# A gated cross-attention and int8 feed-forward block: rows of four batches rounded on GpSimd, turned in 32x32 blocks on VectorE and carried by DMA

## What is computed

```python
def _quant_per_tensor(x):
    scale = jnp.maximum(jnp.max(jnp.abs(x)), MIN_RANGE) / QP      # QP = 127
    return (_ste_round(x / scale), scale)
def _qlinear(x2d, w, b):
    xq, sx = _quant_per_tensor(x2d)
    wq, sw = _quant_per_tensor(w)
    return (jnp.matmul(xq, wq.T) + b[None, :]) * (sw * sx)
x = x + jnp.tanh(g_xattn[0]) * _L0_xattn_ref(_layernorm(x), ctx_1024, ctx_1024, ...)
h = gelu(_qlinear(_layernorm(x), w1, b1))                         # 512 -> 2048
x = x + jnp.tanh(g_ffn[0]) * _qlinear(h, w2, b2)                  # 2048 -> 512
```

## Time and profile before

| | us |
|---|---|
| median of 3 runs | 366.87 (366.56 to 367.69) |
| profiled execution | 366.82 |
| its span, first to last instruction | 365.0 |
| PE busy in the span | 351.0 |
| VectorE busy | 330.1 |
| ScalarE busy | 284.5 |
| GpSimd busy | 119.8 |

### The profile page before, as it was taken

One profiled execution on the slowest core, in us unless ns is written; L12 is line 12 of the kernel. 1 busy time (PEld: TensorE's weight loads), 2 busy tenths in 40 slices (PEclk: granted clock), 3 DMA queues, 4 the chain that ended last, 5 costly groups with the idle time before them and its releaser, 6 DMA issues.

```text
span 365.0 us, 6668 instructions
## 1 busy us (share of the span) xinstructions
PE 351.0 (96%) x2424; PEld 240.0 (66%) x2424; DVE 330.1 (90%) x630; ACT 284.5 (78%) x493; POOL 119.8 (33%) x178
## 2 busy tenths in 40 slices
PE   8889989999999899999999999999999999999995
PEld 2556767887886785454535545454648888888884
DVE  3699999999999969999999888987779999999996
ACT  1476879889886966889859988789799999999520
POOL 2645578688789690079000000430000000000000
PEclk9999999999999999999999999999999999999998
DMA  7999988565311454767738850000192999995225
GB/s 224 370 404 405 396 312 303 193 221 195 116 55 64 171 187 160 291 287 289 330 129 360 331 233 0 3 0 0 58 422 58 371 398 428 423 417 244 95 117 230
DMA packets 22963, 84.78 MB, mean 232 GB/s; under 512 B 2129, under 2 KB 11857, under 8 KB 14482
## 3 DMA queue, kind: packets, MB, share of 16 engines
q1 hardware_dynamic: 22272, 83.89, 59.6%
q10 hardware_dynamic: 658, 0.46, 0.4%
HBM read 54.99 MB, written 29.36 MB: 231 GB/s over the span
## 4 chain that ended last, share of the span: by engine, by line
PE 57%; DVE 20%; ACT 8%; POOL 5%; issue 5%; DMA 3%; SPq 1%; DVEq 0%; ACTq 0%; POOLq 0%
PE PS L1491 19%; PE PS L1446 18%; DVE hmax L1046 6%; PE PS L1327 6%; PE PS L1266 5%; ACT ring L709 5%; DMA X<-in_x 3%; DVE hmax L839 2%; PE PS L1308 2%; PE PS L1275 2%; DVE ring L1023 2%; PE PS L1287 2%; POOL ring L493 2%; POOL w1q L495 1%; PE PS L1298 1%
## 5 line engine op out<-in xcount | busy, mean ns | idle before, releaser
L689 ACT ACTIVATE ring<-PS,bias,sc 128x512 f32<-128x512 f32 x128 | 96.3, 783 | 22.5 <-DVE hmax L1046 6.8
L1446 PE MATMUL PS<-mid,w1q 128*128 128x512 bf16 x500 | 109.8, 379 | 0.6 <-ACT ring L689 0.3
L1446 PEld LDWEIGHTS PS<-mid,w1q 128*128 128x128 bf16 x500 | 48.4, 98 | 58.4 <-ACT ring L689 1.5
L1046 DVE TENSOR_REDUCE hmax<-ring 128x1 f32<-128x2048 f32 x30 | 67.5, 2279 | 5.6 <-ACT ring L689 5.6
L709 ACT ACTIVATE ring<-ring,sc 128x2048 int16<-128x2048 f32 x29 | 55.6, 1987 | 0.0
L1491 PE MATMUL PS<-w2q,ring 128*128 128x256 f16 x336 | 39.0, 273 | 0.0
L1491 PEld LDWEIGHTS PS<-w2q,ring 128*128 128x128 f16 x336 | 32.9, 98 | 4.0
L1174 DVE SCALAR_TENSOR_TENSOR X<-PS,sc,X 128x512 f32<-128x512 f32 x48 | 35.3, 746 | 0.0
L1327 PEld LDWEIGHTS PS<-w2q,ring 128*128 128x128 f32 x256 | 29.2, 192 | 6.7 <-issue 6.7
L1327 PE MATMUL PS<-w2q,ring 128*128 128x128 f32 x256 | 30.5, 277 | 0.4 <-DVE w2q L879 0.4
L1266 PE MATMUL PS<-ring 128*128 128x129 f32 x256 | 30.0, 275 | 0.7 <-ACT ring L612 0.7
(11 more groups left out here) (151 smaller groups left out, 593.4 us busy)
## 6 DMA issues: line engine op xcount, KB each, us to landing
spilled_hidden<-ring SPq DMA_DIRECT2D x20, 1024.0 KB, 3.9
ring<-spilled_hidden SPq DMA_DIRECT2D x20, 1024.0 KB, 9.1
ring<-in_ctxT SPq DMA_DIRECT2D x8, 1024.0 KB, 4.9
ring<-in_ctx SPq DMA_DIRECT2D x8, 896.0 KB, 9.3
X<-in_x SPq DMA_DIRECT2D x7, 1024.0 KB, 9.6
out<-X SPq DMA_DIRECT2D x7, 1024.0 KB, 9.6
ring<-in_w1T SPq DMA_DIRECT2D x4, 1024.0 KB, 13.2
ring<-in_w2T SPq DMA_DIRECT2D x8, 512.0 KB, 3.4
```

The costliest lines, as they stand in the source:

```text
L689: nc.scalar.activation(ring[:, s * CH + c, (h % CH) * N:(h % CH + 1) * N], PS[:, hidden_bank(s, h), :], ACT.Gelu, scale=SC1, bias=bias1[:, ...
L1046: V.tensor_reduce(hmax[:, bass.ds(CH * g + c, 1)], ring[:, s * CH + c, :], AX.X, ALU.max, apply_absolute_value=True).then_inc(hm_done, 1)
L1446: mm = nc.tensor.matmul(PS[:, hidden_bank(s, h), :], w1v[:, k, h * P:(h + 1) * P], xqT[:, s, k, :], start=(k == 0), stop=(k == NH - 1))
```

## The change

For groups 4 to 7 (`CARRIED` is 4) the rows take another way. GpSimd normalises them in float32, adds MAGIC and takes it off (`round_rows`), once group g - 3 is spilled and its maxima are taken. VectorE turns them in 32x32 blocks by four instructions (`turn_x`), between maxima 1 and 2 of group g - 2. SP writes them to HBM (`write_rows`) behind the spills of group g - 2 and fetches them from there in four DMAs (`fetch_rows`), each into 32 partitions, so that every feature stands on its partition. The matmuls of these groups read them in place as [4 x 4 x 32] columns (`turned_block`). TensorE's transposes and VectorE's quantising and copies go for these groups. For group 3 they stay. ScalarE's wait for maxima, at g >= 3, asks for those of group g - 3 only, and falls away below.

```diff
--- before.py
+++ after.py
@@ -46,6 +46,7 @@
     out_v = out.rearrange("b (p i) d -> b p i d", i=NT)
     w1_v = w1T.rearrange("(k p) (a n) -> p k a n", p=P, a=PIECES // NH)
     w2_v = w2T.rearrange("(q k p) n -> q p k n", p=P, q=PIECES)
+    carry = nc.dram_tensor("carried_rows", (B, NT, 32, NT, D), BF16, kind="Internal").ap()
     spill = nc.dram_tensor("spilled_hidden", (SPILLED * CH, P, CW), F32, kind="Internal").ap()
 
     with ExitStack() as es:
@@ -122,6 +123,21 @@
         bpt = mid[:, 1536:2048]
         S_sb = mid[:, 2048:3072].rearrange("p (j e) -> p j e", e=P)
         xqT = mid[:, :].bitcast(BF16).rearrange("p (s k n) -> p s k n", s=SLOTS, k=NH)
+        xqB = mid[:, :].bitcast(BF16).rearrange("p (s t m) -> p s t m", s=SLOTS, t=NT)
+        CARRIED = SLOTS + 1
+
+        def turned_block(g, k):
+
+            return xqB[:, g % SLOTS].rearrange("p t (k i w) -> p k i t w", k=NH, i=NT)[:, k]
+
+        def rounded_rows(g):
+
+            return ring[:, g % SLOTS * CH + 2, 0:CW // 2].bitcast(BF16)
+
+        def turned_rows(g):
+
+            return ring[:, g % SLOTS * CH + 2, CW // 2:CW].bitcast(BF16)
+
         ring16 = ring[:, :, :].bitcast(I16)
         hq = w1q[:, :].bitcast(F16).rearrange("p (c k n) -> p c k n", c=CH, n=N)
         blocks_h = w1q[:, :].bitcast(F16).rearrange("p (c k n) -> p c k n", c=CH, n=HN)
@@ -199,6 +215,9 @@
         w2_step, w2y_done, w2q_done = (sem(n) for n in ("w2_step", "w2y_done", "w2q_done"))
         xs_step, xs_pow, scales = (sem(n) for n in ("xs_step", "xs_pow", "scales"))
         y_done, xq_done, xT_done, xqT_done = (sem(n) for n in ("y_done", "xq_done", "xT_done", "xqT_done"))
+        rounded_g, rounding_g, turned_x = (sem(n) for n in ("rounded_g", "rounding_g", "turned_x"))
+        written = [sem(f"written{g}") for g in range(B)]
+        moved = [sem(f"moved{g}") for g in range(B)]
         h_done, gelu_done, hm_done = (sem(n) for n in ("h_done", "gelu_done", "hm_done"))
         spilled = [sem(f"spilled{s}") for s in range(SLOTS)]
         back_in = [[sem(f"back_in{s}_{c}") for c in range(CH)] for s in range(SLOTS)]
@@ -369,10 +388,31 @@
                 load_w2(q)
 
 
+            def write_rows(g):
+
+                sp.wait_ge(turned_x, NT * (g - CARRIED + 1))
+                sp.dma_start(carry[g].rearrange("t r a m -> (t r) a m"),
+                             turned_rows(g).rearrange("p (a m) -> p a m", a=NT)).then_inc(written[g], 16)
+
+            def fetch_rows(g):
+
+                sp.wait_ge(written[g], 16)
+                sp.wait_ge(h_done, KH * (g - SLOTS + 1))
+                for a in range(NT):
+                    sp.dma_start(xqB[32 * a:32 * a + 32, g % SLOTS],
+                                 carry[g].rearrange("t r a m -> a r t m")[a]).then_inc(moved[g], 16)
+
             for g in range(SPILLED):
                 for c in range(CH):
                     sp.wait_ge(gelu_done, KH * g + (c + 1) * KH // CH + len(H_BANK))
                     sp.dma_start(spill[g * CH + c], ring[:, (g % SLOTS) * CH + c, :]).then_inc(spilled[g % SLOTS], 16)
+                    if c == 0 and g > 2:
+                        fetch_rows(g + 1)
+                if g >= 2:
+                    write_rows(g + 2)
+            fetch_rows(SPILLED + 1)
+            write_rows(B - 1)
+            fetch_rows(B - 1)
 
             for p in range(B):
                 if p + SLOTS < B:
@@ -541,6 +581,24 @@
                 nc.gpsimd.tensor_scalar(w2q[:, q * CW:(q + 1) * CW], w, -MAGIC, 1.0,
                                         ALU.add, ALU.mult).then_inc(w2q_done, 1)
 
+
+            def round_rows(g):
+
+                n = g - CARRIED
+                pool.wait_ge(spilled[g % SLOTS], 16 * CH * (g // SLOTS) + 1)
+                pool.wait_ge(hm_done, CH * (g - SLOTS + 1) + 1)
+                y = ring[:, g % SLOTS * CH + 3, :]
+                for i in range(NT):
+                    nc.gpsimd.tensor_scalar(y[:, i * D:(i + 1) * D], X[:, g, i, :], nmean[:, 4 * g + i:4 * g + i + 1],
+                                            rstd[:, 4 * g + i:4 * g + i + 1], ALU.add, ALU.mult).then_inc(rounding_g, 1)
+                pool.wait_ge(rounding_g, (NT + 1) * n + NT)
+                nc.gpsimd.tensor_scalar(y, y, MAGIC, 1.0, ALU.add, ALU.mult).then_inc(rounding_g, 1)
+                pool.wait_ge(rounding_g, (NT + 1) * (n + 1))
+                nc.gpsimd.tensor_scalar(rounded_rows(g), y, -MAGIC, 1.0, ALU.add, ALU.mult).then_inc(rounded_g, 1)
+
+            pool.wait_ge(xs_step, 8)
+            for g in range(CARRIED, B):
+                round_rows(g)
 
             pool.wait_ge(w2q_done, CH)
             pool.wait_ge(h_done, KH * (B - 2))
@@ -679,8 +737,8 @@
                 act.wait_ge(spilled[s], 16 * CH * turn + 1)
                 for h in range(KH):
                     c = h // (KH // CH)
-                    if h == 0:
-                        act.wait_ge(hm_done, turn * (CH * SLOTS) + 1)
+                    if h == 0 and g >= SLOTS:
+                        act.wait_ge(hm_done, CH * (g - SLOTS + 1) + 1)
                     if g == 1 and h == KH // 2:
                         act.wait_ge(xT_done, 3)
                     if g == 2 and h % (KH // CH) == 0:
@@ -1026,6 +1084,14 @@
                 dve.wait_ge(y_done, 4 * g + 4)
                 V.tensor_copy(xq, yt.rearrange("p i d -> p (i d)")).then_inc(xq_done, 4)
 
+            def turn_x(g):
+
+                dve.wait_ge(rounded_g, g - CARRIED + 1)
+                rows = rounded_rows(g).rearrange("p (i k a w) -> p i k a w", i=NT, k=NH, w=32)
+                out = turned_rows(g).rearrange("p (a k i w) -> p i k a w", a=NT, k=NH, w=32)
+                for i in range(NT):
+                    V.transpose(out[:, i], rows[:, i]).then_inc(turned_x, 1)
+
             def evacuate(g, s):
 
                 dve.wait_ge(xT_done, g + 1)
@@ -1065,14 +1131,16 @@
             V.reciprocal(ISW2, SW2).then_inc(w2_step, 1)
 
             def group(g, s, turn, last):
-                if g > 1 and not last:
+                if g == 2:
                     quantise_x(g + 1, (s + 1) % SLOTS, turn + (s + 1) // SLOTS)
                 group_max(g, s, 0)
                 group_max(g, s, 1)
                 if g == 0:
                     evacuate(2, 2)
-                if g > 1 and not last:
+                if g == 2:
                     evacuate(g + 1, (s + 1) % SLOTS)
+                if 2 <= g < B - 2:
+                    turn_x(g + 2)
                 group_max(g, s, 2)
                 group_max(g, s, 3)
 
@@ -1435,16 +1503,22 @@
                         pe.wait_ge(xqT_done, 3)
                         pe.wait_ge(w2_step, 5)
                         across(4, W2MAX).then_inc(w2_all, 1)
-                    if h == (KH // 2 if g == 0 else KH // 4 if g == 1 else 3 * KH // 4) and not last:
+                    if h == (KH // 2 if g == 0 else KH // 4 if g == 1 else 3 * KH // 4) and g + 1 < CARRIED:
                         if g == 1:
                             pe.wait_ge(w2_step, 6)
                         transposes(g + 1, (s + 1) % SLOTS)
                     pe.wait_ge(gelu_done, KH * g + h + 1)
                     for k in range(NH):
-                        if h == 0 and k % 2 == 0:
+                        if h == 0 and k % 2 == 0 and g < CARRIED:
                             pe.wait_ge(xqT_done, 2 * g + k // 2)
-                        mm = nc.tensor.matmul(PS[:, hidden_bank(s, h), :], w1v[:, k, h * P:(h + 1) * P], xqT[:, s, k, :],
-                                              start=(k == 0), stop=(k == NH - 1))
+                        if h == 0 and k == 0 and g >= CARRIED:
+                            pe.wait_ge(moved[g], 16 * NT)
+                        hidden, w = PS[:, hidden_bank(s, h), :], w1v[:, k, h * P:(h + 1) * P]
+                        if g < CARRIED:
+                            mm = nc.tensor.matmul(hidden, w, xqT[:, s, k, :], start=(k == 0), stop=(k == NH - 1))
+                        else:
+                            mm = nc.tensor.matmul(hidden.rearrange("p (i t w) -> p i t w", i=NT, t=NT), w, turned_block(g, k),
+                                                  start=(k == 0), stop=(k == NH - 1))
                     mm.then_inc(h_done, 1)
 
             groups(pe, group)
```

## The result

The changed kernel takes 363.6 us (median of 6 runs, 363.15 to 364.03) against 366.97 for the one before on the same chips (6 runs). The ratio is 0.9904, with a 95% interval of 0.9894 to 0.9914, so it is 1% or 3.4 us faster. The profiled execution took 363.69 us, its span 361.8. The forecast was faster, with 365.3 us: the direction holds and the time lies in its range, but the gain is 3.4 us and not 1.6.

What follows compares the result with a forecast made beforehand. PE, with VectorE beside it up to batch 2, was taken to bound the hidden layer. 366.82 less 3.89 removed gives 362.93, plus 2.4 for the collision gives 365.3 us; range 362.7 to 368.8.

Steps and rivals of the forecast that it cites:

- What is removed: On PE, the transposes of batches 4 to 7, 3.56 us, and the hole from ScalarE's wait, 0.33 us: 3.89 us.
- The collision: VectorE's quantising of batch 3 alternates with GpSimd's rounding of batch 4, so batch 3 starts 2.4 us later.
- The Trainium skill's rule: VectorE and GpSimd lock their port pair for a whole instruction; one-input passes hold VectorE too, keeping 365.3 us.
- Rival (a): At batch 3's quantising, GpSimd's one-input passes don't hold VectorE up: 362.9 us; chance 0.20.
- Rival (b): GpSimd goes first at batch 3's quantising, which adds 4.2 us: 367.1 us, no change; chance 0.15.
- Rival (c): Carried rows reach PE late at batches 6 and 7: 370.5 us at 1.12 us per turning instruction; chance 0.11.
- The way from turned rows to PE's operand: For a carried batch, the write, three issues and a fetch: 3.4 + 3 x 0.32 + 3.0 = 7.4 us.
- The bound of the lap: Maxima, rounding and turning of a carried batch take 14.0 us a lap against PE's 13.8, with 3.1 us or more in hand.
- Rival (d): Matmuls of batches 4 to 7 read short runs, costing up to 23 ns each: 371.2 us; chance 0.09.
- PE's hole before the transposes: Expected sign: PE idle for some 2.3 us before the batch-3 transposes.

Runs made afterwards that it cites:

- the streams: The kernel before, with eight unused GpSimd passes run through VectorE's quantising of batch 3: 368.11 us with one input, 372.05 us with two.
- the two-input stream: The kernel before, with eight unused two-input GpSimd passes run through VectorE's quantising of batch 3: 372.05 us, ratio 1.0134.

## Why the prediction was right and wrong

- **What is removed:** 3.56 + 0.33 = 3.89 us were forecast, 4.07 measured. ScalarE's wait was worth 0.5 and not the 0.33 that the hole's row gives; 24 matmuls in 5.76 us, where 5.18 are due, would have told.
- **The collision is the step that failed**, as the size of a term: +2.4 us forecast, +0.69 measured in the profiled execution, with place, cause and passage to the end as described (the run without it, and VectorE's lines). Two things were mis-sized. I let every piece but the first wait, and the cast: four holds. There were two, as VectorE's second and third piece went ahead of GpSimd's first pass. Why they did stays open: the pass began 0.29 us behind VectorE's first piece and not 0.1, but with the same 0.29 us only the second piece went ahead in three other traces, and the stretch was 1.14 us. And a hold was put at a whole pass and the piece's tail, 0.765 + 0.28 - 0.457 = 0.59; the streams show pitch + 0.17 - 0.457, 0.47 for this pass, and the two holds cost 0.30 and 0.39. Four holds at 0.47 would be 1.9 us, an estimate; so of the 1.7 us that were too much, 0.5 lie in the price and the rest in the count. With the measured terms the sum is 366.82 - 4.07 + 0.69 = 363.4, against 363.69 for the profiled run. With 1.14 it would be 363.9, which also lies within the six runs (363.15 to 364.03).
- **The Trainium skill's rule** on the exclusive lock, "SBUF — State Buffer", section "SBUF: two separate sides", is borne out as to which pairs meet: passes with one input too, and no maxima (2.28 us beside the two-input stream) or copies from PSUM (0.68 us beside GpSimd's pass at 182.58 in the changed kernel; no run has them beside two inputs). "The other fully blocks" alone doesn't give the price; the order in which a stream of each gets in does. Nor do the recorded starts tell who gets the port: two pieces that started behind GpSimd's pass weren't held.
- **Rival (a)** named 362.9, nearer to the result than the forecast, for a reason that the trace refutes. **Rival (b)** is another order of the same meeting; forced, it gave 369.7 us and not 367.1, part of it by the clock.
- **Rival (c):** 0.60 us an instruction was right, and 3.4 us for a write and 3.0 for a fetch were near (medians 3.1 and 3.0). The way from turned rows to PE's operand was mis-sized: 7.4 us forecast; 9.1, 9.2, 7.8 and 7.0 measured, as SP's issues took up to 1.69 us with the DMA engines full (a share of 1.04 from 190 to 192 us) and fetches up to 4.4 us. So 2.0, 1.6, 2.7 and 3.3 us were in hand for batches 4 to 7 and not 3.6 to 3.1; it cost nothing. The bound of the lap showed when turning was doubled.
- **Rival (d):** the carried matmuls take 55.27 / 256 = 0.216 us (chain of waits, 198.30 to 253.57), as the others do. Runs of 32 columns cost nothing that the trace can show.
- PE's hole before the transposes was 0.29 us and not 2.3, and the clock stayed at full grant there.

## What to carry to other kernels

When work moves to GpSimd, look for VectorE's operations that can be held by it and start on the same semaphore (here the quantising and the cast, from SBUF to SBUF, and not the maxima, the turning or the copies from PSUM). Price the meeting by the number of holds and by the length of a pass, and ask who is first: the same two pieces of work stretched VectorE's by 0.7 or 1.1 us when VectorE was first and by over 4 when GpSimd was, and PE's clock added to that. Either delay one side, or break the chain behind the meeting, as moving a copy ahead of a maximum did here; both gave PE's time back, and both at once only made other rows late. A wait that costs little today (0.5 us here) may be what a reordering needs: try each part of a change with and without the other.

## What was not expected of the hardware

- In a stream against a stream, VectorE's piece and GpSimd's pass alternate, a pair taking the pass's pitch + 0.17 us (0.75 us with passes of 0.58, 0.92 with 0.755, 1.41 with 1.23).
- Where single pieces meet a first pass, the same program text gave two holds in some traces and three in others (0.69 and 1.14 us), with GpSimd 0.29 us behind VectorE in all of them.
- VectorE's 32x32 turning of 128x512 bf16 takes 0.60 us a piece and isn't held by a two-input pass of GpSimd.
- A hole of PE can cost twice. Behind 5.15, 4.01 and 3.20 us the granted clock was 0.50, 0.59 and 0.64 in a window of 4 us that begins within 0.7 us of the hole's end. Behind 2.57 and 2.37 us it was 0.59 and 0.63, behind 2.41 and 2.69 it was 1.00, so the length alone doesn't tell.
- Holding transfers back on a queue for the sake of one urgent write made the writes of the next two batches slower, in two pairs of runs (7.8 against 3.9 us and 7.2 against 3.2 at batch 6) and cost 3.4 and 2.3 us by the ratios. With the backlog the DMA engines' share was 0.93 and 0.85; that this left no room to catch up is my reading.
